# A decoder layer with 160 experts: the table that SyncE reads for each round gets rows of 48 words, read in two register loads

## The chip, the cores and the metric

The kernel runs on one core of a Trainium2 chip. The metric is the device time of one launch in microseconds (us), taken as the median of three runs of the same program.

## The reference

One decoder layer over B = 4 sequences of S = 512 tokens, D = 256. It has three blocks, each with a residual and a layer norm: self-attention with 16 heads, a cross block against a context (one head, a similarity of three terms, a softmax, a product with a 1024x256 matrix), and a mixture of experts. Only the last one bears on the change:

```python
logits = x @ router_w.T + expert_bias[None, :]          # 2048 tokens, 160 experts
probs = jax.nn.sigmoid(logits)
top_w, top_idx = jax.lax.top_k(probs, TOP_K)            # TOP_K = 8
top_w = top_w / (jnp.sum(top_w, axis=-1, keepdims=True) + 1e-09)
top_w = top_w * ROUTED_SCALE
...
h1 = jax.nn.silu(jnp.einsum('th,eih->eti', x, w_gate))  # 256 -> 128 for each expert
h1w = h1 * combine.T[:, :, None]
routed = jnp.einsum('eti,ehi->th', h1w, w_down)         # 128 -> 256
shared = jax.nn.silu(x @ w_gate_shared.T) @ w_down_shared.T
```

All of it is float32.

## The kernel before, in words

There are four stages, each a block of its own with a barrier between: `attend` (attention), `mix` (output projection, cross block, router, and the dispatch of tokens), `experts`, and `combine` (sum of the eight contributions of a token, last layer norm).

**Pages.** `mix` sends each token's row (280 words: the token, its eight weights, destinations and experts' names) by indirect DMAs of GpSimd (POOL) to a pool of rows in HBM (`row_pool`). The pool is cut in pages of 128 rows, and all rows of a page belong to one expert. What page belongs to what expert is known only at run time. VectorE (DVE) works it out at the end of `mix` and writes it as int32 to a table in SBUF, `tables.entry` (`t_entry` in the profile), in the function `fill_tables`.

**Rounds.** `experts` works in rounds, called bodies. A body has 13 entries: 4 of them take two pages of one expert (a pair), 9 take one page, so 17 pages. A body has two halves: half 0 is entries 0 to 6 (9 pages), half 1 is entries 7 to 12 (8 pages). Row number i of `t_entry` belongs to body i. A row is 30 words long before the change: for half 0 seven experts and then nine pages (16 words), for half 1 six experts and then eight pages (14 words). In both kernels `t_entry` starts at an address that is a multiple of 32 bytes but not of 64. Here body 0 is written out, and bodies 1 to 12 run in a loop of six iterations of two bodies each: bodies 1, 3, 5, 7, 9 and 11 are always the first of an iteration.

**The queue of SyncE (SP).** SP computes nothing. It issues the DMAs of an entry in one fixed order. At the first entry of a half `tables.half` (L1419) reads that half's part of the table's row into SP's registers, with one TENSOR_LOAD (L1423) behind one register operation for the address. Then, for each entry, SP waits until TensorE (PE) has transposed the rows that this slot held one ring (13 entries) ago (`turned`), issues one or two loads of a page's rows (L1439, `rows<-row_pool`, 140 KB), waits until PE has done the down projection with the slot's old weights (`downed`), and issues the load of the expert's weights (L1433, `e_w<-w`, 256 KB). The DMA's address is a register from the table, turned into bytes by one more register operation. The waits and the registers' work have no time of their own in the profile's views, the issues have.

**The others.** PE transposes an entry's rows (`e_psx`, L1544), two entries later multiplies them by the gate weights (`e_psg`, L1555), four entries later by the down weights (`e_psy`, L1564). DVE copies the transposed rows (`e_xt`, L1602), and at the second entry of a half it first picks the weights and destinations of all pages of that half (`e_same`, L1578); for that all rows of the half must have arrived. DVE is in order: behind that wait stand the copies on which PE's gate matmuls wait. ScalarE (ACT) does silu and the scaling (`e_y`, L1623), and POOL sends each page's result to `contributions` (L1636).

**Between `mix` and `experts`** SP stands alone for a while: when DVE has written the tables (`tables_done`), SP reads both halves of row 0, issues the first 13 weight loads and the nine row loads of half 0, and comes to the barrier; the other engines wait there.

Of the kernel before, what the change touches and what calls it, by code (L numbers as in the profile page):

```python
# [23 lines left out]
I32 = mybir.dt.int32  # L24
# [5 lines left out]
P = 128  # L30
# [7 lines left out]
EXPERTS, TOP_K, INTER = 160, 8, 128  # L38
# [15 lines left out]
PAIRS, ONES = 4, 9  # L54
PAIRED = (False, True, False, False, True, False, False, False, True, False, False, True, False)
RING_E = PAIRS + ONES
PAGES_E = 2 * PAIRS + ONES
HALVES = 2
ENTRIES_OF = (range(0, 7), range(7, RING_E))
PAGES_OF = (slice(0, 9), slice(9, PAGES_E))  # L60
PAGES = EXPERTS + UNITS
PAIRS_IN = tuple(sum(PAIRED[own.start:own.stop]) for own in ENTRIES_OF)
LISTED_OF = tuple(slice(e.start + p.start, e.stop + p.stop) for e, p in zip(ENTRIES_OF, PAGES_OF))
BODIES = 33
HALF_OF = tuple(int(j >= ENTRIES_OF[1].start) for j in range(RING_E))

# [14 lines left out]
COLUMN, PLACE_OF = (tuple(f(j) for j in range(RING_E)) for f in (column, first_page))  # L81
# [447 lines left out]
class Order:  # L529
# [6 lines left out]
    def do(self, ins):  # L536
        self.n += 1
        ins.then_inc(self.sem, 1)
# [103 lines left out]
def mix(nc, inputs, x, ctx_t, ctx_r, od, rows, place, dispatch, last_sent, tables, w, pool, pool_filled, spent):  # L642
# [8 lines left out]
    with ExitStack() as ctx:  # L651
        sb = lambda n, s, d=F32: ctx.enter_context(nc.sbuf_tensor(n, s, d))
# [16 lines left out]
        st, mv, v, t4 = sb("m_st", [P, TT, 6]), sb("m_mv", [P, TT, 2]), sb("m_v", [P, 2, TT]), sb("m_t4", [P, TT])  # L669
# [15 lines left out]
        low, high, own, scratch = lg, rank, step1, step2  # L685
# [37 lines left out]
        @block.sync  # L723
        def _(sp):
            def load_a(b):

                sp.wait_ge(o_turned, b)
                inputs.load_heads(sp, od[b])
                sp.wait_ge(projected, TT * b)
                sp.dma_start(X[:], x[b]).then_inc(x_in, 16)  # L730

            def load_b(b):

                sp.wait_ge(similar, TT * b)
                sp.dma_start(CT[:], ctx_t[b]).then_inc(ct_in, 16)
                sp.wait_ge(hq_made, DC * b)
                sp.dma_start(CR[:], ctx_r[b]).then_inc(cr_in, 16)

            load_a(1)
            for n in range(B - 2):  # L740
                load_b(n + 1)
                load_a(n + 2)
            load_b(B - 1)
            sp.wait_ge(tables_done, 1)
            listed = [tables.half(0, h) for h in range(HALVES)]
            for j in range(RING_E):
                tables.load_weights(sp, w, j, listed[HALF_OF[j]][0][COLUMN[j]])

            for r in range(2):
                sp.wait_ge(sent[r], (B - r) // 2 * (16 * TT * TOP_K))  # L750
            sp.wait_ge(shared_added, B)
            sp.wait_ge(last_sent, 16 * TT * TOP_K)
            for j in ENTRIES_OF[0]:
                tables.load_rows(sp, pool, j, listed[0][1])

        @block.gpsimd
        def _(pool_eng):
# [297 lines left out]
        def _(dve):  # L1055
# [32 lines left out]
            def step(n, part_b, part_c, part_a):  # L1088
                tile = lambda t: n * TT + (t + 1)
                do1, sync1 = o1.do, o1.sync  # L1090
                do, sync = o2.do, o2.sync
# [196 lines left out]
                def fill_tables():  # L1288
                    dve.wait_ge(tables_spread, 1)
                    full = -(-EXPERTS // ONES)  # L1290
                    in_pairs = lambda i: ps[:, 2, i * P:(i + 1) * P].rearrange("p (h a) -> p h a", a=PAIRS)
                    alone = lambda i: ps[:, 3, i * P:i * P + full * ONES].rearrange("p (h a) -> p h a", a=ONES)
                    pairs_to_here = ones_to_here = 0
                    for h in range(HALVES):
                        own, first = ENTRIES_OF[h], PAGES_OF[h].start
                        pairs_here = sum(PAIRED[own.start:own.stop])
                        ones_here = len(own) - pairs_here
                        listed_here = tables.entry[:, :, LISTED_OF[h]]
                        pairs_own = slice(pairs_to_here, pairs_to_here + pairs_here)
                        ones_own = slice(ones_to_here, ones_to_here + ones_here)  # L1300
                        do(nc.vector.tensor_copy(listed_here[:, 0:P // PAIRS, 0:pairs_here], in_pairs(0)[:, :, pairs_own]))
                        do(nc.vector.tensor_copy(listed_here[:, 0:full, pairs_here:len(own)], alone(0)[:, :, ones_own]))
                        for i in range(2):
                            at = len(own) + i * pairs_here
                            do(nc.vector.tensor_copy(listed_here[:, 0:P // PAIRS, at:at + pairs_here],
                                                     in_pairs(1 + i)[:, :, pairs_own]))
                        do(nc.vector.tensor_copy(listed_here[:, 0:full, len(own) + 2 * pairs_here:], alone(2)[:, :, ones_own]))
                        names = tables.expert[:, 0:P // PAIRS, first:first + 2 * pairs_here].rearrange("p h (a k) -> p h a k", k=2)
                        for i in range(2):
                            do(nc.vector.tensor_scalar(names[:, :, :, i], in_pairs(0)[:, :, pairs_to_here:pairs_to_here + pairs_here],  # L1310
                                                       -1.0, float(EXPERTS), ALU.mult, ALU.add))
                        do(nc.vector.tensor_scalar(tables.expert[:, 0:full, first + 2 * pairs_here:PAGES_OF[h].stop],
                                                   alone(0)[:, :, ones_to_here:ones_to_here + ones_here],
                                                   -1.0, float(EXPERTS), ALU.mult, ALU.add))
                        pairs_to_here, ones_to_here = pairs_to_here + pairs_here, ones_to_here + ones_here
                    sync()
# [91 lines left out]
class Tables:  # L1408
# [3 lines left out]
    def __init__(self, nc, ctx, X):  # L1412
        self.nc, self.X = nc, X
        sb = lambda n, s, d: ctx.enter_context(nc.sbuf_tensor(n, s, d))
        self.entry = sb("t_entry", [P, BODIES, RING_E + PAGES_E], I32)
        self.expert = sb("t_expert", [P, BODIES, PAGES_E], I32)
        self.more = sb("t_more", [P, 1], I32)
        self.W = sb("e_w", [P, RING_E, DC * INTER + D], F32)
        self.w_in, self.x_in = ([ctx.enter_context(nc.semaphore(f"e_{n}_in{r}")) for r in range(RING_E)] for n in "wx")  # L1419

    def half(self, i, h):

        listed = self.nc.values_load_multi_w_load_instructions(  # L1423
            self.entry[0:1, bass.ds(i, 1), LISTED_OF[h]].rearrange("a h e -> a (h e)"), engines=[mybir.EngineType.SP],
            min_val=0, max_val=PAGES - 1,
            skip_runtime_bounds_check_because="every entry is the number of an expert or of a page")[1]
        expert = lambda e: self.nc.s_assert_within(
            e, 0, EXPERTS, skip_runtime_bounds_check_because="every entry is an expert's number or the shared expert's")
        n = len(ENTRIES_OF[h])
        return [expert(e) for e in listed[:n]], listed[n:]  # L1430

    def load_weights(self, sp, w, slot, e):
        return sp.dma_start(self.W[:, slot], w[bass.ds(e, 1)].rearrange("a p n -> (a p) n")).then_inc(self.w_in[slot], 16)  # L1433

    def load_rows(self, sp, pool, slot, pages):
        pairs = PAIRS_IN[HALF_OF[slot]]
# [5 lines left out]
def experts(nc, tokens, tables, w, pool, contrib):  # L1442
# [26 lines left out]
    with ExitStack() as ctx:  # L1469
# [33 lines left out]

        @block.sync
        def _(sp):
            listed = {}

            def step(at):
                h, j = half(at), at_entry(at)
                if j == 0 and not (h == 0 and at.first(RING_E)):  # L1510
                    listed[0] = tables.half(body(at), h)
                if at.first(RING_E):
                    if h > 0:
                        tables.load_rows(sp, pool, at.slot, listed[0][1])
                    return
                v = listed[0][0][COLUMN[at.slot]]
                sp.wait_ge(turned, at.n - (RING_E - 1))
                sp.sem_inc(x_loading, 1)
                if j == 0:
                    sp.wait_ge(picked, at_half(at) - (HALVES - 1))  # L1520
                    sp.sem_inc(x_loading, 1)
                tables.load_rows(sp, pool, at.slot, listed[0][1])

                sp.wait_ge(downed, at.n - (RING_E - 1))
                sp.sem_inc(w_loading, 1)
                tables.load_weights(sp, w, at.slot, v)
            more = run(sp, step, 0)

            for h in range(HALVES):
                sp.wait_ge(sent[h], more * (16 * pages_in[h]) + 16 * pages_in[h])  # L1530
            for n in range(tokens.RING * TT):
                tokens.load(sp, n)
# [309 lines left out]
```

## Time and profile before

| | |
|---|---|
| median of 3 runs | 976.28 us (974.27 to 979.46) |
| span of the profiled execution | 1129.8 us |
| PE busy | 839.3 us (74%) |
| DVE, ACT, POOL busy | 498.1, 414.8, 364.9 us |
| attention | 0 to 288 us |
| `mix` | 288 to about 640 us |
| `experts`, its six iterations | 645 to 1042 us |
| end of `experts`, and `combine` | 1042 to 1129.8 us |

The profiled execution's own time is its span. It is one execution, recorded instruction by instruction, and it is 153.5 us longer than the median of the plain runs; where the record's extra time lies the page does not say. So a count of microseconds in the profile is not at once one in the metric. PE's clock (PEclk) is the share of full speed that was granted in a stretch.

### The profile page before, as it was taken

To read this page: it belongs to the slowest core of one execution; us is meant where nothing else is said; L and a number is where in the kernel's file an instruction comes from. 1 tells how busy PE (TensorE), PEld (TensorE's weight loads), DVE (VectorE), ACT (ScalarE), POOL (GpSimd) and SP (SyncE) were. 2 spreads that over 40 slices of the span, in tenths; PEclk is the share of its full clock that TensorE was granted. 3 is DMA by queue.
4 is the path that set the end of the run, shared out by engine and by line. 5 is a ranking of instruction groups with operands and counts; after the bars stand their busy time and mean duration, and the time that the engine had idled before them with its cause. 6 is when DMAs were issued, how large, how long until landed. Compare 5 with 4: busy or idle time off the path is not lost. (4 is left out here: it accounts for less than half of the span.)

```text
span 1129.8 us, 15900 instructions
## 1 busy us (share of the span) xinstructions
PE 839.3 (74%) x3906; PEld 547.8 (48%) x3906; DVE 498.1 (44%) x1281; ACT 414.8 (37%) x886; POOL 364.9 (32%) x367
## 2 busy tenths in 40 slices
PE   8999999999598983948611386876777767676386
PEld 4433333333356661725411265665565556565275
DVE  1787777772325753545366122222122222222057
ACT  3267777777243341241200133332333333333101
POOL 7000000000000244373737255545455555544400
PEclk9999999999799896977965688888888889888789
DMA  7997878867111222121213677666786767677295
GB/s 252 305 335 263 264 261 265 266 228 258 42 38 37 78 89 90 65 106 44 106 46 140 213 216 215 208 206 205 225 252 191 234 216 225 202 244 207 87 422 196
DMA packets 110272, 213.04 MB, mean 189 GB/s; under 512 B 27735, under 2 KB 58369, under 8 KB 103952
## 3 DMA queue, kind: packets, MB, share of 16 engines
q1 hardware_dynamic: 91616, 175.43, 48.1%
q0 software_dynamic: 16752, 35.20, 8.6%
q10 hardware_dynamic: 1856, 1.84, 0.5%
q8 instruction: 22, 0.36, 0.1%
q14 instruction: 26, 0.21, 0.1%
HBM read 123.35 MB, written 101.19 MB: 199 GB/s over the span
## 5 line engine op out<-in xcount | busy, mean ns | idle before, releaser
L1636 POOL DMA_INDIRECT contributions<-e_y,e_dest x221 | 215.0, 973 | 222.8 <-ACT e_y L1623 161.9
L1555 PE MATMUL e_psg<-e_xt,e_w 128*128 128x128 f32 (+1 forms) x676 | 146.9, 347 | 72.4 <-issue 31.6
L1780 POOL DMA_INDIRECT row_pool<-rows,places x128 | 127.5, 996 | 212.8 <-issue 135.6
L1602 DVE COPY e_xt<-e_psx 128x256 f32<-128x256 f32 (+1 forms) x169 | 84.5, 505 | 202.0 <-PE e_psx L1544 124.4
L516 DVE TENSOR_REDUCE a_mx<-a_psS 128x2 f32<-128x1024 f32 x128 | 152.0, 1218 | 32.4 <-PE a_psS L339 32.2
L1616 ACT ACTIVATE e_g<-e_psg 128x128 f32<-128x128 f32 (+1 forms) x169 | 52.7, 312 | 295.2 <-PE e_psg L1555 196.1
L474 ACT ACTIVATE a_e<-a_psT 128x512 f32<-128x512 f32 x256 | 138.0, 596 | 53.7 <-PE a_psT L369 51.4
L1555 PEld LDWEIGHTS e_psg<-e_xt,e_w 128*128 128x128 f32 x676 | 113.6, 221 | 84.7 <-issue 46.5
L1564 PE MATMUL e_psy<-e_w,e_g 128*128 128x256 f32 x442 | 146.0, 438 | 5.4 <-ACT e_y L1623 5.1
L1544 PE MATMUL e_psx<-m_c,rows 128*128 128x128 f32 x442 | 86.8, 303 | 68.6 <-PEq L651 32.8
L1623 ACT ACTIVATE e_y<-e_psy,e_weight 128x256 f32<-128x256 f32 x221 | 99.1, 474 | 68.1 <-PE e_psy L1564 43.5
L1544 PEld LDWEIGHTS e_psx<-m_c,rows 128*128 128x128 f32 x442 | 63.0, 157 | 101.3 <-issue 59.3
L369 PE MATMUL a_psT<-a_q,a_k 128*128 128x512 f32 x256 | 98.7, 456 | 3.7 <-ACT a_e L474 1.9
L1564 PEld LDWEIGHTS e_psy<-e_w,e_g 128*128 128x128 f32 x442 | 87.2, 222 | 17.0 <-ACT e_y L1623 8.7
L759 POOL MEMSET m_ones<- 128x128 bf16 (+2 forms) x3 | 0.5, 217 | 265.4 <-POOLq L163 265.4
L369 PEld LDWEIGHTS a_psT<-a_q,a_k 128*128 128x128 f32 x256 | 41.2, 187 | 78.3 <-ACT a_e L474 42.2
L380 PE MATMUL a_psO<-a_e,a_v 128*32 128x512 f32 x512 | 68.2, 605 | 0.0
L339 PE MATMUL a_psS<-a_k,a_q 64*128 64x512 f32 x256 | 64.1, 497 | 0.0
L1578 DVE TENSOR_TENSOR e_same<-rows,t_expert 128x72 f32<-128x72 int32 (+1 forms) x26 | 5.9, 229 | 129.6 <-DMA rows<-row_pool 117.1
L339 PEld LDWEIGHTS a_psS<-a_k,a_q 64*128 64x128 f32 x256 | 23.8, 183 | 43.2 <-issue 26.0
L913 PE MATMUL m_ps<-m_at,m_cr 128*128 128x512 f32 x64 | 38.0, 749 | 2.7 <-ACT m_at L1011 2.7
L881 PE MATMUL m_ps<-m_ct,m_et 128*128 128x512 f32 x64 | 35.1, 700 | 6.1 <-ACT m_et L986 6.1
(259 smaller groups left out, 972.9 us busy)
## 6 DMA issues: line engine op xcount, KB each, us to landing
e_w<-w SPq DMA_DIRECT2D x169, 256.0 KB
row_pool<-fill SPq DMA_DIRECT2D x32, 1260.0 KB, 7.2
rows<-row_pool SPq DMA_DIRECT2D x221, 140.0 KB
c_c<-contributions SPq DMA_DIRECT2D x16, 1024.0 KB, 11.7
a_k<-k_parts SPq DMA_DIRECT2D x64, 128.0 KB, 3.3
a_q<-q_parts SPq DMA_DIRECT2D x32, 128.0 KB, 4.1
a_q<-q_parts SPq DMA_DIRECT2D x64, 64.0 KB, 3.4
contributions<-e_y,e_dest POOLq DMA_INDIRECT x221
```

Of the source, the lines that this page charges most:

```text
L339: last = nc.tensor.matmul(psS[:, pair, 1 - u], Q[main(u), at.slot, hh, qt * P:(qt + 1) * P], K[main(u), at.slot, hh], start=True, stop=True)
L369: nc.tensor.matmul(psT[:, BANK[k]], K[:, at.slot, hh, kt * P:(kt + 1) * P], Q[:, at.slot, hh], start=True, stop=True).then_inc(rescored, 1)
L380: last = nc.tensor.matmul(psO[rows], V[:, at.n // NG, kt, head * 2 * DH:(head + 1) * 2 * DH], E[:, kt * HG + hh], start=kt == 0, stop=kt = ...
L474: nc.scalar.activation(E[:, i], psT[:, BANK[i]], ACT.Exp, scale=DH ** -0.5).then_inc(expd, 1)
L516: nc.vector.tensor_reduce(mx[:, at.slot, qt, 2 * DH * pair::HALF], psS[:, pair], AX, ALU.max).then_inc(maxed, 1)
L1544: last = nc.tensor.transpose(ps_x(at, (c * n + k) * P, (c * n + k + 1) * P), X[:, page(at) + k, c * P:(c + 1) * P], ident)
L1555: last = nc.tensor.matmul(ps_g(f, n), W[:, f.slot, c * INTER:(c + 1) * INTER], XT[:, f.slot % XT_RING, c * n:(c + 1) * n], start=c == 0, s ...
L1564: last = nc.tensor.matmul(ps_y(f, k), G[:, f.slot % XT_RING, k * P:(k + 1) * P], W[:, f.slot, DC * INTER:], start=True, stop=True)
L1602: nc.vector.tensor_copy(XT[:, at.slot % XT_RING, 0:n], ps_x(at, 0, n)).then_inc(xt_done, 1)
L1623: nc.scalar.activation(Y[:, page(f) + k], ps_y(f, k), ACT.Copy, scale=weight[:, page(f) + k:page(f) + k + 1]).then_inc(y_done, 1)
L1636: nc.gpsimd.indirect_dma_start(out=contrib, out_offset=bass.IndirectOffsetOnAxis(ap=dest[:, page(f) + k:page(f) + k + 1], axis=0), in_=Y[: ...
L1780: nc.gpsimd.indirect_dma_start(out=pool, out_offset=bass.IndirectOffsetOnAxis(ap=place[:, b, t, k:k + 1], axis=0), in_=rows[:, b, t], in_o ...
```

## The change

A row of the table is now 48 words. Experts of half 0 start at word 0, experts of half 1 at word 8, pages of half 0 at word 16, pages of half 1 at word 32. `tables.half` is replaced by `experts_of` and `pages_of`: two TENSOR_LOADs for a half, of seven and nine words (half 0) or six and eight (half 1). In body 0, whose weights `mix` has loaded, `mix` reads both halves' experts and half 0's pages, and `experts` reads only half 1's pages. DVE writes the same numbers to other columns; its clearing of the table covers 48 in place of 30 words for each of the 33 rows. The tiles that lie behind the table in SBUF move up by 2368 bytes.

```diff
-LISTED_OF = tuple(slice(e.start + p.start, e.stop + p.stop) for e, p in zip(ENTRIES_OF, PAGES_OF))
+EXPERTS_AT, PAGES_AT, LISTED = (0, 8), (16, 32), 48
...
             sp.wait_ge(tables_done, 1)
-            listed = [tables.half(0, h) for h in range(HALVES)]
+            first = [tables.experts_of(0, h, mybir.EngineType.SP) for h in range(HALVES)]
+            first_pages = tables.pages_of(0, 0, mybir.EngineType.SP)
             for j in range(RING_E):
-                tables.load_weights(sp, w, j, listed[HALF_OF[j]][0][COLUMN[j]])
+                tables.load_weights(sp, w, j, first[HALF_OF[j]][COLUMN[j]])
...
-        self.entry = sb("t_entry", [P, BODIES, RING_E + PAGES_E], I32)
+        self.entry = sb("t_entry", [P, BODIES, LISTED], I32)
...
-    def half(self, i, h):
-
-        listed = self.nc.values_load_multi_w_load_instructions(
-            self.entry[0:1, bass.ds(i, 1), LISTED_OF[h]].rearrange("a h e -> a (h e)"), engines=[mybir.EngineType.SP],
-            min_val=0, max_val=PAGES - 1,
...
+    def experts_of(self, i, h, engine):
+
+        return self.nc.values_load_multi_w_load_instructions(
+            self.entry[0:1, bass.ds(i, 1), EXPERTS_AT[h]:EXPERTS_AT[h] + len(ENTRIES_OF[h])].rearrange("a h e -> a (h e)"),
+            engines=[engine], min_val=0, max_val=EXPERTS,
...
+    def pages_of(self, i, h, engine):
+
+        return self.nc.values_load_multi_w_load_instructions(
+            self.entry[0:1, bass.ds(i, 1), PAGES_AT[h]:PAGES_AT[h] + PAGES_OF[h].stop - PAGES_OF[h].start].rearrange(
+                "a h e -> a (h e)"),
...
                 if j == 0 and not (h == 0 and at.first(RING_E)):
-                    listed[0] = tables.half(body(at), h)
+                    if not at.first(RING_E):
+                        numbers[0] = tables.experts_of(body(at), h, mybir.EngineType.SP)
+                    listed[0] = tables.pages_of(body(at), h, mybir.EngineType.SP)
```

On SP, at the head of the loop in `experts`, there stands before (ISA and REGISTER_ALU are register operations; `e_turned`, `e_picked`, `e_downed` are the waits):

```order
316 L1496 COMPARE_AND_BRANCH
317 L1423 ISA
318 L1423 TENSOR_LOAD t_entry
319 L1517 ISA
320 L1520 ISA [waits e_turned]
321 L1439 ISA [waits e_picked]
322 L1439 DMA rows<-row_pool 128x280
323 L1433 ISA [waits e_downed]
324 L1433 DMA e_w<-w 128x512
```

and now, at the same place:

```order
317 L1504 COMPARE_AND_BRANCH
318 L1427 ISA
319 L1427 TENSOR_LOAD t_entry
320 L1434 ISA
321 L1434 TENSOR_LOAD t_entry
322 L1526 ISA
323 L1529 ISA [waits e_turned]
324 L1447 ISA [waits e_picked]
325 L1447 DMA rows<-row_pool 128x280
326 L1441 ISA [waits e_downed]
327 L1441 DMA e_w<-w 128x512
```

One register operation and one load are added in front of the half's first row load; nothing else moves. The same two rows are added at the three other halves of an iteration.

On SP in `mix`, behind the wait for the tables, there stands before:

```order
248 L1423 TENSOR_LOAD t_entry [waits m_tables_done]
249 L1423 TENSOR_LOAD t_entry
250 L1433 ISA
251 L1433 DMA e_w<-w 128x512
252 L1433 ISA
```

and now:

```order
248 L1427 TENSOR_LOAD t_entry [waits m_tables_done]
249 L1427 TENSOR_LOAD t_entry
250 L1434 TENSOR_LOAD t_entry
251 L1441 ISA
252 L1441 DMA e_w<-w 128x512
```

Three loads (7, 6 and 9 words) stand where two were (16 and 14 words). On the other engines the rows and their order are the same, but for the size of one MEMSET.

## Rows read from the trace of the kernel before

**Rows 1.** SP's waits, 640 to 1070 us: what it waited for, total, times, longest.

```profile
SPq L1657 <- DMA contributions<-e_y,e_dest: 15.9, 1, 15.9
```

**Rows 2.** Waits of DVE and of PE's weight loads, same stretch and columns.

```profile
DVE e_same L1578 <- DMA rows<-row_pool: 117.1, 22, 12.1
DVE e_xt L1602 <- PE e_psx L1544: 124.4, 61, 30.2
...
PEld e_psx L1544 <- DMA rows<-row_pool: 28.8, 20, 4.3
```

**Rows 3.** Windows: the stretch before the loop, first and last iteration, the sum.

```profile
core 0: us, PE busy (x) PEld busy (x) DVE busy (x) ACT busy (x) POOL busy (x), PEclk, DMA share, GB/s
611.00:645.00 34.00, 4.33 (x22) 4.19 (x23) 2.91 (x12) 0.47 (x2) 13.91 (x15) 0.52 0.68 218
645.00:714.00 69.00, 54.33 (x287) 45.66 (x286) 18.89 (x55) 25.39 (x70) 36.34 (x38) 0.88 0.72 217
...
974.00:1042.00 68.00, 47.24 (x241) 38.43 (x240) 16.26 (x50) 21.90 (x60) 33.28 (x35) 0.85 0.72 214
sum 431.00, PE 295.62 PEld 241.67 DVE 103.19 ACT 135.55 POOL 216.88; mean PE 42.23 PEld 34.52 DVE 14.74 ACT 19.36 POOL 30.98
```

**Rows 4.** L1423 in bodies 1, 3, 5, 7, 9, 11: ns min/median/max, starts.

```profile
L1423 SPq TENSOR_LOAD <-t_entry x2: 3162/3342/3523, 646.1 to 665.5; - x2
L1423 SPq TENSOR_LOAD <-t_entry x2: 3113/3277/3441, 715.4 to 735.2; - x2
L1423 SPq TENSOR_LOAD <-t_entry x2: 3111/3286/3462, 783.5 to 801.5; - x2
L1423 SPq TENSOR_LOAD <-t_entry x2: 3057/3110/3162, 845.8 to 864.3; - x2
L1423 SPq TENSOR_LOAD <-t_entry x2: 2946/3295/3644, 911.7 to 928.2; - x2
L1423 SPq TENSOR_LOAD <-t_entry x2: 3320/3400/3480, 974.1 to 993.5; - x2
```

**Rows 5.** L1423 in bodies 2, 4, 6, 8, 10, 12.

```profile
L1423 SPq TENSOR_LOAD <-t_entry x2: 1015/1106/1197, 682.9 to 701.8; - x2
L1423 SPq TENSOR_LOAD <-t_entry x2: 296/732/1169, 750.1 to 770.3; - x2
L1423 SPq TENSOR_LOAD <-t_entry x2: 610/898/1185, 818.2 to 833.2; - x2
L1423 SPq TENSOR_LOAD <-t_entry x2: 986/1084/1181, 880.3 to 896.7; - x2
L1423 SPq TENSOR_LOAD <-t_entry x2: 984/1260/1536, 944.9 to 960.8; - x2
L1423 SPq TENSOR_LOAD <-t_entry x2: 986/1083/1180, 1008.5 to 1029.2; - x2
```

**Rows 6.** The table's load and its address operation for body 0; the one-word load.

```profile
L1423 SPq TENSOR_LOAD <-t_entry x2: 1361/1388/1416, 611.3 to 612.6; - x2
L1423 SPq TENSOR_LOAD <-t_entry x1: 1169/1169/1169, 640.3 to 640.3; - x1
...
L1423 SPq FUSED_REGOPS  x24: 4/46/75, 646.0 to 1029.1; - x24
...
L1492 SPq TENSOR_LOAD <-t_more x1: 281/281/281, 639.7 to 639.7; - x1
```

**Rows 7.** Timeline of SP before the loop, and in a quick piece of it.

```profile
614.25 20.18 SPq L1433 DMA_DIRECT2D e_w<-w  x13
634.76 16.29 SPq L1439 DMA_DIRECT2D rows<-row_pool  x18
...
706.75 0.33 SPq L1439 DMA_DIRECT2D rows<-row_pool  x1
707.34 0.33 SPq L1433 DMA_DIRECT2D e_w<-w  x1
708.00 0.86 SPq L1439 DMA_DIRECT2D rows<-row_pool  x1
709.13 0.33 SPq L1433 DMA_DIRECT2D e_w<-w  x1
709.79 0.86 SPq L1439 DMA_DIRECT2D rows<-row_pool  x2
710.91 0.33 SPq L1433 DMA_DIRECT2D e_w<-w  x1
711.65 0.25 SPq L1439 DMA_DIRECT2D rows<-row_pool  x1
```

**Rows 8.** The clearing of the table, and what DVE waits for after it.

```profile
290.17 0.88 DVE L1063 MEMSET t_entry<- 128x990 int32 x1 [0.15 <-issue]
...
296.81 0.76 DVE L555 BATCH_NORM_STATS2 m_st<-m_ps 128x6 f32<-128x256 f32 x2 [5.17 <-PE m_ps L815]
```

More of the change, by code:

```diff
@@ L62 @@
 PAIRS_IN = tuple(sum(PAIRED[own.start:own.stop]) for own in ENTRIES_OF)
-LISTED_OF = tuple(slice(e.start + p.start, e.stop + p.stop) for e, p in zip(ENTRIES_OF, PAGES_OF))
+EXPERTS_AT, PAGES_AT, LISTED = (0, 8), (16, 32), 48
+assert len(ENTRIES_OF[0]) <= EXPERTS_AT[1] and len(ENTRIES_OF[1]) <= PAGES_AT[0] - EXPERTS_AT[1]
+assert all(own.stop - own.start <= 16 for own in PAGES_OF)
 BODIES = 33
@@ L753, in _ @@
             for j in ENTRIES_OF[0]:
-                tables.load_rows(sp, pool, j, listed[0][1])
+                tables.load_rows(sp, pool, j, first_pages)
         @block.gpsimd
@@ L1297, in fill_tables @@
                         ones_here = len(own) - pairs_here
-                        listed_here = tables.entry[:, :, LISTED_OF[h]]
+                        experts_here = tables.entry[:, :, EXPERTS_AT[h]:EXPERTS_AT[h] + len(own)]
+                        pages_here = tables.entry[:, :, PAGES_AT[h]:PAGES_AT[h] + 2 * pairs_here + ones_here]
                         pairs_own = slice(pairs_to_here, pairs_to_here + pairs_here)
                         ones_own = slice(ones_to_here, ones_to_here + ones_here)
-                        do(nc.vector.tensor_copy(listed_here[:, 0:P // PAIRS, 0:pairs_here], in_pairs(0)[:, :, pairs_own]))
-                        do(nc.vector.tensor_copy(listed_here[:, 0:full, pairs_here:len(own)], alone(0)[:, :, ones_own]))
+                        do(nc.vector.tensor_copy(experts_here[:, 0:P // PAIRS, 0:pairs_here], in_pairs(0)[:, :, pairs_own]))
+                        do(nc.vector.tensor_copy(experts_here[:, 0:full, pairs_here:], alone(0)[:, :, ones_own]))
                         for i in range(2):
-                            at = len(own) + i * pairs_here
-                            do(nc.vector.tensor_copy(listed_here[:, 0:P // PAIRS, at:at + pairs_here],
+                            at = i * pairs_here
+                            do(nc.vector.tensor_copy(pages_here[:, 0:P // PAIRS, at:at + pairs_here],
                                                      in_pairs(1 + i)[:, :, pairs_own]))
-                        do(nc.vector.tensor_copy(listed_here[:, 0:full, len(own) + 2 * pairs_here:], alone(2)[:, :, ones_own]))
+                        do(nc.vector.tensor_copy(pages_here[:, 0:full, 2 * pairs_here:], alone(2)[:, :, ones_own]))
                         names = tables.expert[:, 0:P // PAIRS, first:first + 2 * pairs_here].rearrange("p h (a k) -> p h a k", k=2)
@@ L1419, in __init__, with load_weights @@
         self.w_in, self.x_in = ([ctx.enter_context(nc.semaphore(f"e_{n}_in{r}")) for r in range(RING_E)] for n in "wx")
-    def half(self, i, h):
-        listed = self.nc.values_load_multi_w_load_instructions(
-            self.entry[0:1, bass.ds(i, 1), LISTED_OF[h]].rearrange("a h e -> a (h e)"), engines=[mybir.EngineType.SP],
-            min_val=0, max_val=PAGES - 1,
[L1426 to L1433, printed above, removed]
+    def experts_of(self, i, h, engine):
+        return self.nc.values_load_multi_w_load_instructions(
+            self.entry[0:1, bass.ds(i, 1), EXPERTS_AT[h]:EXPERTS_AT[h] + len(ENTRIES_OF[h])].rearrange("a h e -> a (h e)"),
+            engines=[engine], min_val=0, max_val=EXPERTS,
+            skip_runtime_bounds_check_because="every entry is an expert's number or the shared expert's")[1]
+    def pages_of(self, i, h, engine):
+        return self.nc.values_load_multi_w_load_instructions(
+            self.entry[0:1, bass.ds(i, 1), PAGES_AT[h]:PAGES_AT[h] + PAGES_OF[h].stop - PAGES_OF[h].start].rearrange(
+                "a h e -> a (h e)"),
+            engines=[engine], min_val=0, max_val=PAGES - 1,
+            skip_runtime_bounds_check_because="every entry is the number of a page")[1]
+    def load_weights(self, eng, w, slot, e):
+        return eng.dma_start(self.W[:, slot], w[bass.ds(e, 1)].rearrange("a p n -> (a p) n")).then_inc(self.w_in[slot], 16)
     def load_rows(self, sp, pool, slot, pages):
@@ L1505, in _ @@
         def _(sp):
-            listed = {}
+            listed, numbers = {}, {}
             def step(at):
@@ L1510, in step @@
                 if j == 0 and not (h == 0 and at.first(RING_E)):
-                    listed[0] = tables.half(body(at), h)
+                    if not at.first(RING_E):
+                        numbers[0] = tables.experts_of(body(at), h, mybir.EngineType.SP)
+                    listed[0] = tables.pages_of(body(at), h, mybir.EngineType.SP)
                 if at.first(RING_E):
                     if h > 0:
-                        tables.load_rows(sp, pool, at.slot, listed[0][1])
+                        tables.load_rows(sp, pool, at.slot, listed[0])
                     return
-                v = listed[0][0][COLUMN[at.slot]]
                 sp.wait_ge(turned, at.n - (RING_E - 1))
@@ L1521, in step @@
                     sp.sem_inc(x_loading, 1)
-                tables.load_rows(sp, pool, at.slot, listed[0][1])
+                tables.load_rows(sp, pool, at.slot, listed[0])
                 sp.wait_ge(downed, at.n - (RING_E - 1))
                 sp.sem_inc(w_loading, 1)
-                tables.load_weights(sp, w, at.slot, v)
+                tables.load_weights(sp, w, at.slot, numbers[0][COLUMN[at.slot]])
             more = run(sp, step, 0)
```

## The prediction

> **What bounds the kernel now.** I read the waits of SP first, over the stretch of the experts [rows 1]. In 430 us the view lists one wait of SP, at the very end. None on PE is listed, though SP asks for `turned` and `downed` at every entry: what it asks for has nearly always happened already. SP does not run ahead of the others, it runs behind them. Then I read who waits for SP's transfers: DVE's pick waits 117.1 us in 22 of 26 halves for the rows of its half, and PE waits 28.8 us more for rows directly [rows 2]. While DVE waits in the pick, the copies behind it are late and PE's gate matmuls with them. Last I read the windows. In the 397 us of the six iterations (63 to 69 us each; the first and the last stand in the rows) PE is busy 291 us (the sum 295.6 less the 4.3 of the stretch before), so 48.6 us of about 66 in an iteration, at 0.85 to 0.88 of its clock, and DMA about 0.7 busy [rows 3]. Nothing is full. In this execution the chain of SP's issues sets the pace, and what SP does before a half's first row load delays all rows of the half.
>
> **The loads before.** The durations of L1423 fall in two kinds. In odd bodies the 12 loads take 2946 to 3644 ns [rows 4], in sum 39.4 us. In even bodies the 12 take 296 to 1536 ns [rows 5], in sum 12.3 us. The number of words is the same in both. What differs is the address. A row is 30 words, 120 bytes, so an odd row starts 8 bytes past a multiple of 16, and an even row on a multiple of 16; 16 words further, where half 1 starts, it is the same. Body 0 is even, and its loads take 1361, 1416 and 1169 ns [rows 6]. A count of pieces fits. If an aligned run of four words is one piece and any other word is one, then 16 aligned words are 4 pieces, 14 aligned are 5 (three runs, two words), and unaligned they are 16 and 14. With 185 ns and 200 ns for a piece this gives 985, 1185, 3385 and 2985 ns. The rows have 984 to 1015 for the 16 words (two are shorter), 1169 to 1197 for the 14 (one is longer), and means of 3380 and 3190 unaligned. The one-word load has 281 ns, the form gives 385. The form is my reading of the rows; both parts are estimates.
>
> The Trainium skill ("Runtime: NRT & Kernel Launch", Instruction fetch mechanics) states about 200 ns for a register in a load, even for many. The odd bodies agree (3380 / 16 = 211 ns), the even ones do not (985 / 16 = 62 ns).
>
> **The loads after.** A row is 192 bytes, and all four parts start on a multiple of 32 bytes in every body. By the form: seven experts are 4 pieces, 985 ns; nine pages 3 pieces, 785; six experts 3, 785; eight pages 2, 585. A body takes 3.14 us. Now the sum:
> - loop, before: 39.4 + 12.3 = 51.7 us;
> - loop, after: 12 x 3.14 = 37.7, and 24 added address operations at 46 ns [rows 6] with a gap before and behind, say 0.1 us each, 2.4: 40.1 us. That is -11.6 us. An odd body gains 6.57 - 3.14 - 0.2 = 3.2, an even one loses 3.14 + 0.2 - 2.05 = 1.3;
> - `mix`: three loads 985 + 785 + 785 = 2.56 us for 2.78, so -0.2. This stands on the path: SP goes on at 614.25 with 13 weight loads and the row loads of half 0, and PE is busy for 4.33 us of the 34 [rows 3, 7];
> - body 0, half 1: 585 for 1169 ns, -0.6;
> - DVE: the clearing goes from 990 to 1584 words, 0.88 to 1.41 us, +0.5. Behind it DVE waits 5.17 us for PE [rows 8], so this costs nothing; were that cover gone, 0.5 us;
> - `fill_tables`: as many elements in as many copies, with another stride: nothing, for they read PSUM just as before. The tiles that moved keep their alignment to 32 bytes, and no transfer changes its size: nothing.
>
> In sum -12.4 us on SP. No price of a load of 6 to 9 words stands in the trace. From below a load costs the 281 ns of the one-word load: 4 x 0.28 + 0.2 = 1.3 us for a body, 16 for the loop, -36 us. From above it costs what its half's load costs at the same place now: +51.7 + 2.4 = +54 us. The form lies on the rows with most in common (the same table, many words, aligned), so I take it.
>
> **From SP to the time.** In the profiled execution the queue bounds, the saving is whole, and the sum is 1129.8 - 12.4 = 1117 us. The plain runs are 153.5 us shorter, and there SP may be less of a bound. SP's own quick pace is 1.25 us for a one-page entry (706.75 to 708.00) and 1.86 or less for a pair (709.79 to 711.65) [rows 7]; with 18 of the one and 8 of the other an iteration is 22.5 + 14.9 = 37.4, and with 8.6 of loads 46.0 us. PE's busy 48.6 us would be 41.8 at full clock. Had the six iterations taken their share of the 153.5 us in the 461 us from 611 to 1072, they would run at 44 us each: there SP binds and all is gained. Were the difference spread over the whole program, an iteration would take 57 us, and the loads would bind only where they come in a lump, at the start of odd bodies: 6.6 us in front of rows for which DVE waits. So between none and all of 12.4. I take two thirds, 8.3 us: 976.3 - 8.3 = 968.
>
> **The rivals.** (Below 0.5%, about 4.9 us, a measurement of this kernel can't tell a change from none.)
>
> *A, the forecast:* shorter loads on the queue that binds, 962 to 971 us, gain of over 0.5%. Chance 0.60, with the case of cheaper loads (down to 281 ns; PE then binds sooner, some 20 us gained at most, 956) in it.
>
> *B, SP is not the bound in a plain run.* For it: it is 153.5 us shorter, and in the record many issues of SP take far longer than the quick 0.33 us (13 weight issues spread over 20.18 us [rows 7]), which may be the record's own doing. PE's 48.6 us of an iteration is more than SP's 46.0. Then the loads are hidden behind PE's work, up to the lumps, and the time is 972 to 977, say 975. Against it: DVE waits for rows in 22 of 26 halves. Chance 0.22.
>
> *C, a load is paid by the register.* The words are as many as before (30 in a body), so the loads cost the same, and the two added address operations of a body, 12 x 0.2 = 2.4 us, are all: 976.3 + 1.6 to 2.4, 978. Against it: 62 and 211 ns for a word of the same table. Chance 0.07. The figure of about 200 ns for a register in the Trainium skill ("Runtime: NRT & Kernel Launch", Instruction fetch mechanics) comes to this rival.
>
> *D, slower: the load is long by its place in the loop, not by its address.* Odd bodies are always the first copy in the loop, so rows 4 can't tell the one from the other. Then a load at an odd place takes 3.3 us for seven words as for sixteen, an even one 1.0, and the 24 added ones cost 51.7 + 2.4 = 54 us of SP, of which two thirds are 36: 1012 us. It decides from a mean load of (51.7 - 2.4) / 48 = 1.03 us on: above that the new kernel's loads cost more than the old ones'. Against it: the second slow load of an iteration stands some 20 us behind the branch, the one-word load takes 281 ns, and neither place has anything else in common. A milder form is that a load has a floor near 1 us: about 48 us for 48 loads, no loss yet. With lesser losses of this kind, chance 0.11.
>
> **How the numbers follow.** Faster by over 0.5% is A: 0.60. Within 0.5%: B and C, and the mildest of D: 0.30. Slower: the rest of D, 0.10. The range reaches from the cheaper loads of A, 957, to beyond C, 980: A, B and C whole, with D outside, and a part of A's lower tail. A's own range is 962 to 971. Predicted is A's, 968.
>
> **What would show it.** In the profile after: the loads of odd and of even bodies take the same time, seven words about 985 ns, nine and six about 785, eight about 585, and their sum in the loop is 38 us in place of 51.7. The iterations are about 2 us shorter each. DVE's wait for rows falls from 117 us by some 5 to 12. If the loads are as said but the time stays, B is right. If odd places stay above 2 us, D is. I would be wrong also if the shorter stall of SP only moves the row and weight transfers closer together, so that each lands later: then DVE's wait stays at 117 with the loads down.

## The result, and the profile of the changed kernel

The changed kernel takes 962.67 us, median of 4 runs (959.42 to 963.59), beside 975.27 us (973.69 to 979.46, 4 runs) for the kernel before. The ratio is 0.9855, with a 95% interval of 0.9828 to 0.9883: 12.6 us faster as medians (by the ratio 14.1 us, and between 11.4 and 16.8).

The page of its profiled execution (core 0; busy time and its share of the span; tenths in 40 slices):

```profile
span 960.9 us, 15949 instructions
PE 794.5 (83%) x3906; PEld 526.2 (55%) x3906; DVE 499.5 (52%) x1281; ACT 421.9 (44%) x886; POOL 369.1 (38%) x367
...
PEclk9999999999996998999889656989999999998599
DMA  6998886887451110333222266999999999995593
```

This span, 960.9 us, belongs to an execution that was timed at 962.69 us. So a record adds next to nothing to a run, and the 153.5 us by which the first record of the kernel before was longer than its plain runs has another reason. The experiments below found it: there are two conditions under which this program runs. Under the one it takes 975 us before the change (the runs of the result), under the other some 1125 to 1135 us (the three chips, numbers 7, 11 and 14, that ran the experiments). The first record was of the second kind, the record of the changed kernel is of the first. Whether the condition goes with the chip or with something else isn't shown: the chip of the result's runs is not on record, and each of the three chips showed the second condition alone. What follows compares within one kind, or says that it can't.

The two loads in the changed kernel, L1427 (experts) and L1434 (pages), min/median/max in ns:

```profile
L1427 SPq TENSOR_LOAD <-t_entry x26: 740/1072/1352, 560.5 to 862.8; - x26
L1427 SPq FUSED_REGOPS  x24: 46/56/75, 592.1 to 862.7; - x24
...
L1434 SPq TENSOR_LOAD <-t_entry x26: 529/764/1098, 562.9 to 863.8; - x26
```

The same two in narrow windows: `mix` for body 0, body 0's half 1, and half 0 of body 1 and of body 2:

```profile
L1427 SPq TENSOR_LOAD <-t_entry x2: 975/1164/1352, 560.5 to 561.9; - x2
L1434 SPq TENSOR_LOAD <-t_entry x1: 749/749/749, 562.9 to 562.9; - x1
...
L1434 SPq TENSOR_LOAD <-t_entry x1: 534/534/534, 587.1 to 587.1; - x1
...
L1427 SPq TENSOR_LOAD <-t_entry x1: 945/945/945, 592.2 to 592.2; - x1
L1434 SPq TENSOR_LOAD <-t_entry x1: 751/751/751, 593.3 to 593.3; - x1
...
L1427 SPq TENSOR_LOAD <-t_entry x1: 943/943/943, 617.0 to 617.0; - x1
L1434 SPq TENSOR_LOAD <-t_entry x1: 791/791/791, 618.1 to 618.1; - x1
```

Seven words take 945 ns in an odd body and 943 in an even one. The two kinds of [rows 4, 5] are gone: added up from the trace, the 24 loads of odd bodies make 22.0 us, the 24 of even bodies 21.6.

Windows of the stretch before the loop and of the six iterations (same columns as [rows 3]):

```profile
558.00:591.00 33.00, 3.61 (x16) 3.53 (x17) 4.64 (x24) 0.28 (x1) 16.56 (x18) 0.54 0.72 237
592.00:641.00 49.00, 44.32 (x268) 38.82 (x267) 17.89 (x53) 25.53 (x67) 34.08 (x35) 0.93 0.90 291
...
827.00:873.00 46.00, 40.59 (x238) 35.40 (x237) 16.16 (x50) 22.71 (x60) 32.88 (x35) 0.93 0.95 310
sum 314.00, PE 250.50 PEld 218.20 DVE 104.44 ACT 141.45 POOL 216.97; mean PE 35.79 PEld 31.17 DVE 14.92 ACT 20.21 POOL 31.00
```

An iteration takes 281 / 6 = 46.8 us here. PE is busy 41.1 us of it (250.5 less 3.6, by six), at 0.93 to 0.96 of its clock, and DMA is 0.90 to 0.95 busy at 291 to 310 GB/s, where the first record, under the second condition, had 66 us, 0.7 and some 215 GB/s.

Who waits, 585 to 900 us:

```profile
DVE e_same L1587 <- DMA rows<-row_pool: 91.0, 24, 7.4
...
SPq L1666 <- DMA contributions<-e_y,e_dest: 15.3, 1, 15.3
SPq L1539 <- DMA contributions<-e_y,e_dest: 2.8, 1, 2.8
```

As in [rows 1, 2], SP waits for nothing inside the loop (L1539 stands behind it), and DVE's pick waits for rows, in 24 of 26 halves.

The timeline of SP at the head of the loop:

```profile
596.90 0.86 SPq L1447 DMA_DIRECT2D rows<-row_pool  x2
598.02 0.33 SPq L1441 DMA_DIRECT2D e_w<-w  x1
598.68 0.33 SPq L1447 DMA_DIRECT2D rows<-row_pool  x1
...
600.36 0.34 SPq L1447 DMA_DIRECT2D rows<-row_pool  x1
600.96 0.33 SPq L1441 DMA_DIRECT2D e_w<-w  x1
601.63 0.33 SPq L1447 DMA_DIRECT2D rows<-row_pool  x1
```

A pair costs SP 1.78 us (596.90 to 598.68), a single entry 1.27 us (600.36 to 601.63). Eight of the one and 18 of the other make 14.2 + 22.9 = 37.1 us; the loads are 43.6 / 6 = 7.3, and their eight address operations with gaps about 0.8. That is 45.2 of an iteration's 46.8 us. SP's own work fills 97% of the loop. The trace says the same directly: between two instructions of SP in the loop there is never a gap of more than 0.37 us.

DMA is nearly as full, so the rival that full DMA queues hold SP up in its issues has to be looked at. The durations of all its issues (min/median/max in ns):

```profile
L1447 SPq DMA_DIRECT2D rows<-row_pool x221: 317/333/344, 581.5 to 872.4; - x111
L1441 SPq DMA_DIRECT2D e_w<-w x169: 332/333/1447, 563.8 to 873.0; - x169
```

Of the 360 issues in the loop three take more than 0.4 us (1447, 1321 and 1062 ns), all others 0.32 to 0.34. So SP is not held up, and its own work is the bound in this record.

Before the loop it is not. Between the 13 weight issues and the first row load SP waits for the last rows that `mix` scatters (same columns as [rows 1], 558 to 650 us):

```profile
SPq L755 <- DMA row_pool<-rows,places: 9.5, 1, 9.5
```

So under this condition the table's loads in `mix` have 9.5 us of cover.

### The profile page after: what moved, and what is told of

Its sections match the earlier page's. It is cut to its first block and busy times, and to the rows that moved or that the text cites. A ratio compares the mean times of both kernels' runs of the same rounds, so it can differ in the third digit from the quotient of the medians.

```text
span 960.9 us, 15949 instructions
## 1 busy us (share of the span) xinstructions
PE 794.5 (83%) x3906; PEld 526.2 (55%) x3906; DVE 499.5 (52%) x1281; ACT 421.9 (44%) x886; POOL 369.1 (38%) x367
## 5 line engine op out<-in xcount | busy, mean ns | idle before, releaser
L1789 POOL DMA_INDIRECT row_pool<-rows,places x128 | 131.4, 1026 | 160.0 <-issue 136.0
L518 DVE TENSOR_REDUCE a_mx<-a_psS 128x2 f32<-128x1024 f32 x128 | 152.0, 1218 | 32.4 <-PE a_psS L341 32.2
L1564 PE MATMUL e_psg<-e_xt,e_w 128*128 128x128 f32 (+1 forms) x676 | 136.2, 327 | 37.3 <-DVE e_xt L1611 31.5
L1573 PE MATMUL e_psy<-e_w,e_g 128*128 128x256 f32 x442 | 130.2, 398 | 0.0
L1564 PEld LDWEIGHTS e_psg<-e_xt,e_w 128*128 128x128 f32 x676 | 104.9, 206 | 44.9 <-DVE e_xt L1611 35.1
L1553 PE MATMUL e_psx<-m_c,rows 128*128 128x128 f32 x442 | 79.4, 283 | 32.8 <-PEq L653 30.3
L1553 PEld LDWEIGHTS e_psx<-m_c,rows 128*128 128x128 f32 x442 | 60.1, 146 | 53.7 <-issue 32.1
L1573 PEld LDWEIGHTS e_psy<-e_w,e_g 128*128 128x128 f32 x442 | 80.3, 204 | 6.3
```

Source lines behind the costliest of these rows:

```text
L518: nc.vector.tensor_reduce(mx[:, at.slot, qt, 2 * DH * pair::HALF], psS[:, pair], AX, ALU.max).then_inc(maxed, 1)
L1553: last = nc.tensor.transpose(ps_x(at, (c * n + k) * P, (c * n + k + 1) * P), X[:, page(at) + k, c * P:(c + 1) * P], ident)
L1564: last = nc.tensor.matmul(ps_g(f, n), W[:, f.slot, c * INTER:(c + 1) * INTER], XT[:, f.slot % XT_RING, c * n:(c + 1) * n], start=c == 0, s ...
L1573: last = nc.tensor.matmul(ps_y(f, k), G[:, f.slot % XT_RING, k * P:(k + 1) * P], W[:, f.slot, DC * INTER:], start=True, stop=True)
L1789: nc.gpsimd.indirect_dma_start(out=pool, out_offset=bass.IndirectOffsetOnAxis(ap=place[:, b, t, k:k + 1], axis=0), in_=rows[:, b, t], in_o ...
```

## What differs between the two conditions

The register operations of SP before the weight loads, in the changed kernel's record of the result (first fence) and in a record of the kernel before on chip 14 (`e1_before_again`, second fence):

```profile
L1441 SPq FUSED_REGOPS  x169: 37/43/47, 563.7 to 872.8; - x169
L1441 SPq MOVE e_w<-w x169: 29/29/29, 563.8 to 872.9; - x169
```

```profile
L1433 SPq FUSED_REGOPS  x169: 2/43/712, 618.2 to 1046.4; - x169
L1433 SPq MOVE e_w<-w x169: 2/29/727, 618.3 to 1046.4; - x169
```

The medians are alike, the longest are not. An operation that sets one register takes 29 ns every time in the one, up to 727 ns in the other. SP's quick pace is the same in both (1.25 us for an entry in [rows 7], 1.27 here). The rest is long operations and, more of it, pauses between two instructions of SP in which nothing is recorded. Counted from the traces, the loop of the first record has 126 pauses of over 0.5 us, 88 us in sum, and `e1_before_again` 111, 79 us; the changed kernel under the first condition has none. Both appear where SP issues weight and row loads: 13 weight issues spread over 20.18 us in [rows 7], and over 7.88 us in the record of the result:

```profile
563.83 7.88 SPq L1441 DMA_DIRECT2D e_w<-w  x13
```

SP is not the whole difference. The changed kernel ran under both conditions (960.9 us here, 1125.1 us in `f1_changed_again`, 164 us more). The loop takes 281.1 and 394.3 us of it, so 113 us of the difference. But the first load of the table starts at 560.5 us in the one and at 610.5 in the other, and attention ends at about 288 in both: 50 us are lost in `mix`, before SP reads the table at all. PE has long waits there that the first condition doesn't have (400 to 600 us; record of the result, then `f1_changed_again`):

```profile
PE m_ps L911 <- DVE m_g L1359: 2.3, 2, 1.1
```

```profile
PE m_ps L911 <- DVE m_g L1359: 26.7, 2, 15.3
PE m_ps L850 <- DVEq L1151: 11.7, 1, 11.7
```

In every record of the second condition PE waits over 11 us at a time at these two places (L908 and L847 in the kernels without the change); in the record of the result it is 2.4 us at most. What makes the operations long, and what stops the engines in `mix`, no run showed.

## The experiments

All twelve ran on chips of the second condition. Where an expectation has two numbers, the one for 1132 us is the one that was put to the test; where it has only the numbers for 975 us, it is its difference in SP's time and its load durations that can be read.

**The kernel before again** (no edit).

> The kernel before, unchanged, for a second profile of it, since the first one's span (1129.8 us) is 17% over the plain runs. If the record itself made that execution long, this span is again near 1130 us. If that one execution was disturbed, the span is near 973 us, as the changed kernel's record lies within 2 us of its plain time. The loads then still have their two kinds: about 3.2 us in odd bodies, 1.0 to 1.2 us in even ones, some 51 us in the loop.

Measured: 1137.67 us, span 1135.9, median of the kernel before on that chip 1132.75 (23 runs). Neither alternative was right as put: the span is near 1130, and so are the unrecorded runs. The record costs nothing; the condition does. The loads have their two kinds: 40.2 us in odd bodies and 10.4 in even ones, 50.5 in sum. Body 2, which had 1015 and 1197 ns in [rows 5]:

```profile
L1423 SPq TENSOR_LOAD <-t_entry x2: 995/1088/1181, 690.1 to 707.2; - x2
```

**Shift by two words: is it the address or the place?**

```diff
-LISTED_OF = tuple(slice(e.start + p.start, e.stop + p.stop) ...)
+LISTED_OF = tuple(slice(2 + e.start + p.start, 2 + e.stop + p.stop) ...)
-        self.entry = sb("t_entry", [P, BODIES, RING_E + PAGES_E], I32)
+        self.entry = sb("t_entry", [P, BODIES, 34], I32)
```

> The kernel before with rows of 34 words of which the first two are unused: odd bodies now start on a multiple of 16 bytes, even ones 8 bytes past it. Address theory: the slow loads (3.0 to 3.4 us) move to the even bodies, the quick ones (985 and 1185 ns) to the odd; the loop's sum stays near 51 us, body 0 gets the slow ones (+3.6 us in mix, +1.8 us in its half 1), and the time is 975 + 5 = 980 us. Place theory (the first copy in the loop is slow whatever the address): odd bodies stay slow, even ones quick, time 975 us.

Measured: ratio 0.9998 (0.9971 to 1.0025). Bodies 1 to 4, in four windows:

```profile
L1423 SPq TENSOR_LOAD <-t_entry x2: 1001/1034/1068, 648.5 to 666.7; - x2
L1423 SPq TENSOR_LOAD <-t_entry x2: 1907/2578/3250, 681.9 to 704.3; - x2
L1423 SPq TENSOR_LOAD <-t_entry x2: 869/1205/1541, 718.5 to 735.4; - x2
L1423 SPq TENSOR_LOAD <-t_entry x2: 3287/3554/3822, 745.8 to 766.9; - x2
```

The slow loads moved to the even bodies (37.0 us there, 12.4 in the odd ones). The code and its place in the loop are the same, only the address changed, so it is the address. Body 0's three loads did grow, from 3.95 to 10.5 us, but the time did not (the interval reaches to +2.8 us). The trace shows where `mix` got its part back: from SP's first table load to its first row load it is 23.7 us here, 23.5 in the first record and 23.2 in `e1_before_again`, because the 13 weight issues between them took 15.6 us in place of 20.2 and 19.8.

**All loads off.** Rows of 36 words, numbers from word 2 on; the diff is that of the shift with 36 for 34.

> The kernel before with rows of 36 words, the numbers from word 2 on: every load starts 8 bytes past a multiple of 16. Address theory: all 24 loads of the loop take 3.4 or 3.0 us, 76 us in sum for 51, and body 0 adds 5.4: +30.6 us on SP. If SP's queue bounds the plain runs, the time is 975 + 30 = 1005 us; if PE or DMA does, less than half of it, below 990 us. Place theory: no change, 975 us.

Measured: ratio 1.0105 (1.0063 to 1.0147), 1145.44 us, +12.7. All loads of the record are slow, odd and even (median 3355 ns, none under 2220):

```profile
L1423 SPq TENSOR_LOAD <-t_entry x27: 2220/3355/4054, 612.9 to 1044.6; - x27
```

Two repeats, meant for the other condition:

> Rows of 36 words with every load 8 bytes off, on a chip where the kernel before takes 975 us: +30.6 us on SP, 1005 us if SP's queue bounds the loop whole; less than 990 if it does in part. Where it takes 1132 us: +12 us again.

> Rows of 36 words with every load 8 bytes off, once more. Where the kernel before takes 975 us: +30 us, ratio 1.031, if the queue of SP binds the loop whole, half of that or less if it does in part. Where it takes 1133 us: ratio 1.0105 as twice before.

They gave 1.0105 (1.0037 to 1.0173) on chip 11 and 1.0073 (1.0036 to 1.011) on chip 14. The direction is clear of 1 three times. The size is +12.7, +9.4 and +5.4 us as medians (the last +3.2 without its three longest runs): a tenth to four tenths of the 30.6 us.

**One load, rows of 32 words: is it the alignment or the split?**

```diff
-        self.entry = sb("t_entry", [P, BODIES, RING_E + PAGES_E], I32)
+        self.entry = sb("t_entry", [P, BODIES, 32], I32)
```

> The kernel before with rows of 32 words and nothing else: one load for a half as before, half 0 at word 0, half 1 at word 16, each on a multiple of 32 bytes. Theory (pieces of four aligned words, 185 + 200 ns for each piece): 985 and 1185 ns in every body, 26 us in the loop for 51, so 975 - 25 = 950 us, 12 us less than the changed kernel: the alignment gave all and the second load took part of it back. Rival, that short loads are what helped: then this is 975 us. Rival, that DMA (0.99 busy in the changed kernel's record) is the next bound: then it stays at 962 us.

> Rows of 32 words and one load for a half, beside the changed kernel. On a chip where the kernel before takes 975 us: SP binds, so the 25 us of loads come off whole, 950 us, ratio 0.974. If DMA bounds the changed kernel (0.99 busy in its record), 962 us, ratio 0.986 as for the changed kernel. On a chip where it takes 1132 us: ratio 0.993 again.

Measured: 0.9931 (0.9901 to 0.9961) on chip 14 and 0.9933 (0.9897 to 0.997) on chip 11. This alone, without the split, makes the kernel faster, by 7.6 and 9.0 us. (The 0.99 for DMA in the expectation is too high: the six windows of the changed kernel have 0.90 to 0.95.)

**The changed kernel** on the second condition:

> The changed kernel, beside the kernel before on one chip. Where the kernel before takes about 975 us and SP's register operations take their quick 30 to 50 ns: ratio 0.986, 962 us. Where it takes about 1132 us and many of SP's register operations take 700 ns: by the loads (-12 us on SP) and the third of a microsecond for each that the runs with other rows gave there, -4 us, ratio 0.996.

Measured: 0.9946 (0.9914 to 0.9979) on chip 11, -8.0 us as medians.

**The split alone**, from the old rows:

```diff
-EXPERTS_AT, PAGES_AT, LISTED = (0, 8), (16, 32), 48
+EXPERTS_AT, PAGES_AT, LISTED = (0, 16), (7, 22), 30
```

> The split alone: the changed kernel's two loads for a half from the old rows of 30 words (experts at words 0 and 16, pages at 7 and 22). Theory of aligned pieces: a load that starts off a multiple of 16 bytes pays for every word, so 5.5 us a body, 69 us in the loop for 51, +19 us in all: 994 us where the kernel before takes 975. If an unaligned load used runs of four once it reaches them: 3.7 us in even bodies, about the changed kernel's. Rival, that the split itself is the gain: 962 us or below. In the trace: nine pages near 2.0 us, eight near 1.8 in even bodies.

Measured: 1.0032 (0.9992 to 1.0072): no gain; a loss is likely but not clear of 1. Nine pages from word 7 in `mix`, eight from word 22 in body 0:

```profile
L1433 SPq TENSOR_LOAD <-t_entry x1: 2136/2136/2136, 615.1 to 615.1; - x1
...
L1433 SPq TENSOR_LOAD <-t_entry x1: 1679/1679/1679, 641.5 to 641.5; - x1
```

The same nine and eight words take 749 and 534 ns in the changed kernel, from words 16 and 32 (751 and 535 in `f1_changed_again`, on the same chip as this run). A load that starts off the 16 bytes doesn't pick up the aligned runs further on: the count with them would have been 785 ns for the nine.

**Sixteen words for both halves: is it the number of words?** On top of the rows of 32:

```diff
-            self.entry[0:1, bass.ds(i, 1), LISTED_OF[h]].rearrange("a h e -> a (h e)"), engines=[mybir.EngineType.SP],
+            self.entry[0:1, bass.ds(i, 1), 16 * h:16 * h + 16].rearrange("a h e -> a (h e)"), engines=[mybir.EngineType.SP],
```

> Rows of 32 words, one load for a half, and half 1 too reads 16 words instead of 14 (two unused ones more). By the pieces, half 1's load takes 4 pieces in place of 3 runs and 2 words: 985 ns for 1185, so more words in less time, and 23.6 us in the loop for 26. A price by the register would give more, not less. Against the kernel before: where it takes 975 us and SP binds, -28 us, ratio 0.971; where it takes 1133 us, ratio 0.992.

Measured: 0.9889 (0.9849 to 0.9929) on chip 14. The load of body 0's half 1, one instruction at one place, with 14 words (first fence, the record of `e4_one_load_rows_32`) and with 16 words (second fence, this kernel):

```profile
L1423 SPq TENSOR_LOAD <-t_entry x1: 1169/1169/1169, 640.1 to 640.1; - x1
```

```profile
L1423 SPq TENSOR_LOAD <-t_entry x1: 975/975/975, 637.9 to 637.9; - x1
```

Two words more, 194 ns less. That is what the count of pieces says, and a price by the register can't give it.

**Side by side**, on chip 7:

> Rows of 32 words, one load of sixteen words for each half, once more and directly beside the changed kernel. Its loads take 24 us in the loop where the changed kernel's take about 38 when nothing stretches them, and body 0 is alike. Where the kernel before takes 975 us: 947 us, 15 us below the changed kernel. Where it takes about 1133 us: 1122 us, 5 us below the changed kernel, as a third of the loads' time is what such a chip gives back.

> The changed kernel beside it: 962 us where the kernel before takes 975 (ratio 0.986), 1128 us where it takes about 1133 (ratio 0.995).

Measured: 0.9906 (0.9873 to 0.9938) and 0.9927 (0.9894 to 0.996), with 1112.5 and 1114.3 us. The two intervals overlap, so the single load is not shown to be the better one, only no worse. Under the first condition it wasn't run.

The kernels in a table; the second column is the change of SP's time from the count of pieces, worked out before the runs (the changed kernel: the sum of the prediction), the third the change of the medians beside the kernel before on the same chip:

| kernel | on SP, us | time, us | ratios |
|---|---|---|---|
| sixteen words, both halves | -28 | -13.7, -11.9 | 0.9889, 0.9906 |
| rows of 32, one load | -25 | -7.6, -9.0 | 0.9931, 0.9933 |
| the changed kernel | -12.4 | -8.0, -10.1 | 0.9946, 0.9927 |
| shifted by two words | +5 | +0.7 | 0.9998 |
| the split alone | +19 | +4.8 | 1.0032 |
| all off | +30.6 | +12.7, +9.4, +5.4 | 1.0105, 1.0105, 1.0073 |
| the changed kernel, first condition | -12.4 | -12.6 | 0.9855 |

The time follows the load time in sign and nearly in order, but under the second condition with only about a third of it (from -28 to +30.6 on SP, 58.6 us, the time goes from about -12.8 to +9.2, 22 us, 0.37). Under the first condition, in the one kernel that was timed there, the time fell by as much as the sum says.

The loads as the traces have them, against the kernel before (51.7 and 50.5 us in the loop), and the pauses of over 0.5 us in the loop (77 to 88 us in the kernels with the old load time):

| kernel | loads of the loop, us | pauses, us |
|---|---|---|
| sixteen words, both halves | 18.3, 18.8 | 99, 90 |
| rows of 32, one load | 23.7, 23.0 | 92, 89 |
| the changed kernel | 32.2, 34.3 | 89, 83 |
| before, shifted by two words | 51.7, 50.5, 49.5 | 88, 79, 77 |
| the split alone | 64.6 | 86 |
| all off | 77.6, 78.0, 80.5 | 65, 75, 65 |

The shorter the loads, the more time SP spends in pauses. This is where a part of the gain goes: some 60 us of loads between the first and the last row of this table are met by some 26 us of pauses the other way. That the pauses follow from the loads, and by what, is not shown.

## Why the prediction was right, point by point

- **SP's chain of issues sets the pace: right in the changed kernel's record, not shown whole for the kernel before.** SP's own work is 97% of an iteration there, without a gap and without a held-up issue. The experiments changed little but SP's loads and moved the time both ways, but all under the second condition, where the pauses of SP take 77 to 88 us of the loop. The prediction met these pauses only in its rival B. (The clock of the six iterations is 0.84 to 0.90 in that record, not 0.85 to 0.88.) The tiles that the change moves are no likely cause: two rows of other lengths moved them too, by some 0.5 KB with no change of the time (the shift) and by some 0.8 KB with a slower kernel (all off). That DMA, up to 0.95 busy, would become the bound with still shorter loads is open, since no kernel with shorter loads ran under the first condition.
- **The loads cost by address: right, and shown.** The shift settles it against the place in the loop (rival D), and the sixteen words settle it against a price by the register (rival C). The form of 185 + 200 ns for each piece is a little high: the shortest loads measured are 943 ns for seven words, 749 for nine, 740 for six and 529 for eight, where it gave 985, 785, 785 and 585. A run of four words as one piece fits all of these; that the chip really fetches so is my reading.
- **The sum, two terms off.** The loop's loads are 43.6 us in the record after, not 37.7: some are as short as above, others of the same size take up to 1317, 1098, 1233 and 956 ns (in the same order; why is open). With the added address operation, 0.108 us from one load's end to the next one's start, that is 46.2 us for 40.1. Against the 51.7 us of the first record the loop gives -5.5, and with `mix` and body 0 the sum would be about -6 us, half of what was measured. The loads of the kernel before may be longer too under the first condition, and then the sum is larger; there is no record of them there. So the 12.6 us measured can't be split, and that it falls on the sum's 12.4 is luck as far as the records go.
- **`mix`: wrong in sign, small, and not on the path.** The three loads take 1352 + 975 + 749 = 3.08 us, not 2.56, for 2.78 before: the first load behind the wait and the second are longer there than in the loop, in every record (1361 and 1416 ns in [rows 6]). The prediction put them on the path; in the record after, SP then waits 9.5 us for scattered rows, which covers them. Body 0's half 1 gains 0.64 us (534 for 1169).
- **DVE's clearing: right.** 1.38 us for 0.88 (1.41 expected), and hidden: two instructions later DVE still waits 4.29 us for PE:

```profile
289.75 1.38 DVE L1066 MEMSET t_entry<- 128x1584 int32 x1 [0.28 <-issue]
...
296.01 0.76 DVE L557 BATCH_NORM_STATS2 m_st<-m_ps 128x6 f32<-128x256 f32 x2 [4.29 <-PE m_ps L818]
```

- **"I take two thirds": the weak step.** The factor came from reading the 153.5 us as the record's own cost, or as something of SP that a plain run would not have. The first was wrong, the second held only for plain runs of the first condition. The record was of the other condition, where register operations of SP take up to 0.7 us. Where the metric was taken, SP has none of these and its pace is regular, so nothing there speaks for taking less than the whole. The time fell by 12.6 us in place of 8.3, at the edge of A's own range of 962 to 971; whether that is all that the loads lost can't be said, as above. Under the condition of the first record it was taken as whole (-12.4 to 1117 us), and there 8 to 10 us came, from 1124 and 1135.
- **Rival B** (hidden behind PE) is out: PE is busy 41.1 of 46.8 us (it had been taken as 48.6 from the other condition's record), SP all of it, and the time fell.
- **DVE's wait for rows** was to fall by 5 to 12 us. Under the second condition I have it in single records only: 117.1 and 108.7 us before (the first record, and chip 14), 113.9 and 125.9 for the changed kernel (chips 11 and 7). It did not fall there. That is the sign the prediction named for being wrong, the loads down and the wait still near 117. Under the second condition it came, beside a smaller gain and longer pauses of SP; under the first the changed kernel has 91.0 us and the kernel before no record. The iterations were to be 2 us shorter each; the loop has 394.3 and 377.2 us for 393.5 and 396.9 before, on different chips, and can't show that either.

## What to carry to other kernels

When a sequencer reads a table into registers inside a loop that is bound by its issues, look at the duration of the same load in successive rounds. If it alternates, look at the row's length modulo 16 bytes: padding a row from 30 to 32 words is a change of one number. And before a record's span is reasoned with, compare it with the plain times of the same chip: a gap of 16% was a different condition, not an overhead.

## What was not expected of the hardware

The same program took 975 us in the runs of the result and 1116 to 1144 us on chips 7, 11 and 14, with equal work. In the slow case SP's register operations of 29 to 43 ns sometimes take 700 ns, from the first weight loads of the expert stage on, while the median stays, and it pauses as long between operations; `mix` is 50 us longer before that. A register load of eight aligned words took 534 ns and one of eight words 8 bytes off 1679 ns; sixteen words took 975 ns aligned and about 3.4 us off.
